# Cross attention for 16 batches: 718 keys in five tiles of 128 rows and one of 78, with the last tile's three products stacked into two

## The reference

```
query = hidden_states @ Wq                    # 100 x 640 per batch
keyt  = enc @ Wk                              # 718 x 640
valt  = enc @ Wv
scores = einsum('bhqd,bhkd->bhqk', qh, kh) * d ** -0.5
probs  = softmax(scores)
hs     = einsum('bhqk,bhkd->bhqd', probs, vh)
out    = (hs + ca_hs2) @ Wout + b_out + residual
```

## Time and profile before

| | |
|---|---|
| three runs | 1013.64 us median (1012.01 to 1024.04) |
| profiled execution | 1011.86 us, span 1010.1 us |
| TensorE (PE) busy | 988.2 us, 98% of the span |
| VectorE busy | 677.8 us, 67% |
| ScalarE busy | 489.2 us, 48% |
| GpSimd busy | 343.7 us, 34% |
| DMA | 190.12 MB, 188 GB/s on average |
| mean granted TensorE clock | 0.994 of full speed |

### The profile page before, as it was taken

The page is one execution under the profiler, slowest core; times in us unless marked ns, Lnnn a source line. Parts: engine busy times, 40 slices in busy tenths (PEclk is TensorE's granted clock), DMA queues, the critical chain, the costliest instruction groups (busy, mean ns, idle before and its releaser), DMA issues.

```text
span 1010.1 us, 20729 instructions
## 1 busy us (share of the span) xinstructions
PE 988.2 (98%) x6740; PEld 959.7 (95%) x6740; DVE 677.8 (67%) x1129; ACT 489.2 (48%) x895; POOL 343.7 (34%) x286
## 2 busy tenths in 40 slices
PE   9999899999999999999999999999999999999998
PEld 8998799999999999999999999999999999998997
DVE  6445586767776767676767776777767676766444
ACT  7434455454554545454636363645454545446110
POOL 5212253334242515161615243343333343406000
PEclk9999999999999999999999999999999999999999
DMA  7989967787879777879697878787787877795354
GB/s 264 255 298 272 250 154 198 157 201 168 189 167 195 169 191 171 183 176 186 169 186 184 187 176 190 178 184 187 166 201 162 199 169 190 156 219 160 98 177 148
DMA packets 154169, 190.12 MB, mean 188 GB/s; under 512 B 80928, under 2 KB 108192, under 8 KB 154144
## 3 DMA queue, kind: packets, MB, share of 16 engines
q1 hardware_dynamic: 147456, 177.44, 73.5%
q10 hardware_dynamic: 6688, 12.35, 3.7%
HBM read 81.56 MB, written 19.95 MB: 100 GB/s over the span
## 4 chain that ended last, share of the span: by engine, by line
PE 78%; DMA 7%; SPq 5%; DVE 4%; issue 2%; ACT 2%; POOL 1%; ACTq 0%; DVEq 0%; POOLq 0%
PE psS L750 20%; PE psB L785 19%; PE psB L790 9%; PE psS L725 7%; PE psT L766 6%; PE psS L894 6%; PE psT L812 4%; PE psT L818 2%; SPq L382 2%; DMA kstack<-kT 2%; DMA enc_raw<-in_encN_dram 1%; SPq L379 1%; PE psB L867 1%; PE psB L844 1%; PE psT L819 1%
## 5 line engine op out<-in xcount | busy, mean ns | idle before, releaser
L750 PE MATMUL psS<-encT_keep,Wk_keep 128*128 128x360 f32 x1440 | 253.8, 329 | 0.0
L750 PEld LDWEIGHTS psS<-encT_keep,Wk_keep 128*128 128x128 f32 x1440 | 237.4, 188 | 1.1 <-issue 0.4
L785 PE MATMUL psB<-PT_h,encN_h 120*128 120x400 f32 x576 | 202.3, 351 | 0.0
L785 PE MATMUL psB<-PT_l,encN_h 120*128 120x400 f32 x576 | 198.8, 345 | 0.0
L1133 ACT ACTIVATE probs<-psS,negmax 100x718 f32<-100x718 f32 x128 | 110.2, 861 | 133.5 <-DVE negmax L1524 133.4
L612 POOL TENSOR_TENSOR encT_keep<-encT_raw,encT_keep 128x718 fp32r<-128x718 f32 x45 | 79.7, 1772 | 199.6 <-ACT encT_keep L1162 197.3
L1548 DVE TENSOR_TENSOR kT<-psS,kT 128x718 fp32r<-128x718 f32 x80 | 72.4, 905 | 85.7 <-ACT kT L1157 85.6
L620 POOL TENSOR_TENSOR encN_l<-enc_raw,encN_h 120x768 fp32r<-120x768 f32 x48 | 93.1, 1940 | 90.9 <-ACT encN_h L1169 89.9
L790 PE MATMUL psB<-PT_h,encN_l 120*128 120x400 f32 x576 | 120.3, 344 | 0.8 <-POOL encN_l L620 0.8
L603 POOL TENSOR_TENSOR Mbd<-Mbd,fmask 128x320 fp32r<-128x320 f32 x48 | 46.7, 973 | 218.0 <-DMA Mbd<-m_split 215.4
L1157 ACT ACTIVATE kT<-psS 128x718 fp32r<-128x718 f32 x80 | 61.7, 771 | 115.7 <-PE psS L750 102.5
(11 more groups left out here) (245 smaller groups left out, 1642.2 us busy)
## 6 DMA issues: line engine op xcount, KB each, us to landing
kstack<-kT SPq DMA_DIRECT2D x64, 448.8 KB
kstack<-kT SPq DMA_DIRECT2D x192, 112.2 KB
enc_raw<-in_encN_dram SPq DMA_DIRECT2D x48, 360.0 KB, 5.5
encT_raw<-in_encT_dram SPq DMA_DIRECT2D x45, 359.0 KB, 4.4
kstack<-kT SPq DMA_DIRECT2D x32, 359.0 KB
kstack<-kT SPq DMA_DIRECT2D x32, 269.2 KB
kstack<-kT SPq DMA_DIRECT2D x32, 179.5 KB, 3.2
kstack<-kT SPq DMA_DIRECT2D x64, 89.8 KB, 3.5
```

The lines of the kernel that those rows point to most:

```text
L750: mm = pe.matmul(keys_in(f, first)[:, half, 0:HALF], w[:, c, f * 128:(f + 1) * 128], e[:, c, k0:k0 + HALF], start=(j == 0), stop=(j == 3 * ...
L785: pe.matmul(psB[:, 1, 0:RH], eN[0][:, k, cc], PT[p][:, k, rows], start=(k == 0 and p == 0), stop=False)
```

## The change

KP, the rows of a key tile, becomes 128 (KPAD 768), and the last tile holds 78 keys (TAIL). HALF, the width of a score half, stays 360. In a unit of `context` the first five tiles keep their 15 products. The three products of the last tile become two of 117 rows: the first takes high `encN` by high `PT` in rows 0 to 77 and, in rows 78 to 116, the first 39 rows of low `encN` by the first 39 of high `PT`; the second takes high `encN` by low `PT` and, in rows 78 to 116, the other 39 rows of low by high.

The rows 78 to 116 are filled by DMA, issued by SyncE in its order: `tail_pt` twice a batch (two DMAs of 39 rows x 400 columns each) and `tail_enc` once (two DMAs of 39 rows x 384 and one of 78 rows x 384). GpSimd makes the low part of the last tile first, in place in `enc_raw`, then of tile 4, then of tiles 0 and 1, 2 and 3. TensorE waits for `entail` and `pttail` ahead of the sixteenth matmul of a unit. At the end, GpSimd splits two parts of Wout instead of three ahead of the last `enc_low`, and `tail_pt(B - 1, 1)` stands ahead of the last stores and loads.

```
-KP = (KEYS + KT - 1) // KT
+KP = 128
 KPAD = KT * KP
-HALF = KPAD // 2
+HALF = 360
+FULLK = KEYS // KP
+TAIL = KEYS - FULLK * KP
+TH = TAIL // 2
+TSTK = TAIL + TH
...
+        tail_low = enc_raw[0:KP, FULLK * C:KT * C].bitcast(F32R)
...
+        def third(c):
+            return slice(4, 6) if c == 0 else slice(2 * (c - 1), 2 * c)
...  load_enc
-                    free("encN", PARTS * (b - 1) + c + 1, first)
-                    ks = slice(c * KQ, (c + 1) * KQ)
+                    free("encN", LOWS * (b - 1) + c + 2, first)
+                    if c == 0:
+                        free("entail", 48 * b, first)
+                    ks = third(c)
...
+                def tail_pt(b, half):
+                    wait_apart(sp, s["ptlo"], HEADS * b + 4 * half + 4, s["passed_sp"])
+                    rows = slice(half * RH, (half + 1) * RH)
+                    for p in range(2):
+                        sp.dma_start(raw(PT[p][TAIL:TSTK, FULLK, rows]),
+                                     raw(PT[0][p * TH:(p + 1) * TH, FULLK, rows])).then_inc(s["pttail"], 16)
+                def tail_enc(b):
+                    wait_apart(sp, s["encN"], LOWS * b + 1, s["passed_sp"])
+                    for p in range(2):
+                        sp.dma_start(raw(eN[p][TAIL:TSTK, FULLK, :]), raw(tail_low[p * TH:(p + 1) * TH, :]))\
+                          .then_inc(s["entail"], 16)
+                    sp.dma_start(raw(eN[1][0:TAIL, FULLK, :]), raw(eN[0][0:TAIL, FULLK, :])).then_inc(s["entail"], 16)
...  batch of SyncE, behind load_encT(i + 1, 1)
                     if not first:
+                        tail_pt(i - 1, 1)
                         store_hs(i - 1, 0)
...  batch of SyncE, behind load_x(i + 1)
                     if first:
                         sp.wait_ge(s["encT"], PARTS)
                         sp.dma_start(wv_raw, tiled(Wv)).then_inc(s["wvin"], 16)
                         load_q(i + 1)
-                    else:
+                    tail_pt(i, 0)
+                    tail_enc(i)
+                    if not first:
                         wait_apart(sp, s["hsp"], 2 * i, s["passed_sp"])
                         load_v2(i)
...  SyncE, the end
                 for t in range(2):
                     load_tile(0, t)
+                tail_pt(B - 1, 1)
                 store_hs(B - 2, 1)
...  enc_low of GpSimd
+                    pool.wait_ge(s["encNhi"], PARTS * b + 1)
+                    nc.gpsimd.tensor_tensor(tail_low, rawN[:, FULLK, :], eN[0][:, FULLK, :],
+                                            ALU.subtract).then_inc(s["encN"], 1)
+                    nc.gpsimd.tensor_tensor(eN[1][:, FULLK - 1, :], rawN[:, FULLK - 1, :], eN[0][:, FULLK - 1, :],
+                                            ALU.subtract).then_inc(s["encN"], 1)
...  context of TensorE
-                    for k in range(KT):
+                    for k in range(FULLK):
                         for p in range(2):
                             pe.matmul(psB[:, 1, 0:RH], eN[0][:, k, cc], PT[p][:, k, rows],
                                       start=(k == 0 and p == 0), stop=False)
-                    for k in range(KT):
-                        if u == 0 and k % KQ == 0:
-                            pe.wait_ge(s["encN"], PARTS * i + k // KQ + 1)
-                        mm = pe.matmul(psB[:, 1, 0:RH], eN[1][:, k, cc], PT[0][:, k, rows],
-                                       start=False, stop=(k == KT - 1))
-                    mm.then_inc(s["u"], 1)
+                    for n, k in enumerate((4, 0, 1, 2, 3)):
+                        if u == 0 and n in (0, 1, 3):
+                            pe.wait_ge(s["encN"], LOWS * i + (n + 1) // 2 + 2)
+                        pe.matmul(psB[:, 1, 0:RH], eN[1][:, k, cc], PT[0][:, k, rows], start=False, stop=False)
+                    if u == 0:
+                        pe.wait_ge(s["entail"], 48 * i + 48)
+                    if c == 0:
+                        pe.wait_ge(s["pttail"], 64 * i + 32 * half + 32)
+                    pe.matmul(psB[:, 1, 0:RH], eN[0][0:TSTK, FULLK, cc], PT[0][0:TSTK, FULLK, rows],
+                              start=False, stop=False)
+                    pe.matmul(psB[:, 1, 0:RH], eN[1][0:TSTK, FULLK, cc], PT[1][0:TSTK, FULLK, rows],
+                              start=False, stop=True).then_inc(s["u"], 1)
```

More of the change, by code:

```diff
@@ L109, in program @@
         NP = FT + 1
+        LOWS = PARTS + 1
         HALFCOLS = slice(GT, 2 * GT)
@@ L249, in program @@
         splits = "encT encN gbd ahi a xhi xlo v2bd mbd wolo passed_sp passed_pool"
+        tails = "pttail entail"
         stage1_loads = "xT0 xT1 xT2 xT3 xT4 wqin0 wqin1 wqin2 wqin3 wqin4 wgin cain wkcain wvcain wkin encin wvin hin"
@@ L256, in program @@
         stage1_stores = "qst0 qst1 qst2 qst3a qst3b v2st mst0 mst1 mst2"
-        names = " ".join((loads, products_done, exps_and_highs, steps_and_lows, splits, stage1_loads, stage1,
+        names = " ".join((loads, products_done, exps_and_highs, steps_and_lows, splits, tails, stage1_loads, stage1,
                           stage1_stores)).split()
@@ L547, in _ @@
                 batch(B - 1, last=True)
-                sp.wait_ge(s["encN"], PARTS * B)
+                sp.wait_ge(s["encN"], LOWS * B)
                 for t in range(2):
                     load_tile(0, t)
+                tail_pt(B - 1, 1)
                 store_hs(B - 2, 1)
@@ L616, in enc_low @@
                 def enc_low(b):
-                    for c in range(PARTS):
-                        ks = slice(c * KQ, (c + 1) * KQ)
+                    pool.wait_ge(s["encNhi"], PARTS * b + 1)
+                    nc.gpsimd.tensor_tensor(tail_low, rawN[:, FULLK, :], eN[0][:, FULLK, :],
+                                            ALU.subtract).then_inc(s["encN"], 1)
+                    pool.wait_ge(s["encN"], LOWS * b + 1)
+                    nc.gpsimd.tensor_tensor(eN[1][:, FULLK - 1, :], rawN[:, FULLK - 1, :], eN[0][:, FULLK - 1, :],
+                                            ALU.subtract).then_inc(s["encN"], 1)
+                    pool.wait_ge(s["encN"], LOWS * b + 2)
+                    for c in range(1, PARTS):
+                        ks = third(c)
                         pool.wait_ge(s["encNhi"], PARTS * b + c + 1)
@@ L621, in enc_low @@
                                                 ALU.subtract).then_inc(s["encN"], 1)
-                        pool.wait_ge(s["encN"], PARTS * b + c + 1)
+                        pool.wait_ge(s["encN"], LOWS * b + c + 2)
                 def spread_v2(b):
@@ L698, in wo_low @@
                     pool.wait_ge(s["wolo"], c + 1)
-                for c in range(3):
+                for c in range(2):
                     wo_low(c)
                 enc_low(B - 1)
-                for c in range(3, FT):
+                for c in range(2, FT):
                     wo_low(c)
```

## The result

| | before | after |
|---|---|---|
| median | 1014.28 us (1012.01 to 1024.04, 4 runs) | 1067.43 us (1064.1 to 1071.72, 4 runs) |
| ratio | | 1.0528, interval 1.0483 to 1.0573 |
| profiled execution | 1011.86 us, span 1010.1 | 1064.1 us, span 1062.4 |
| mean granted TensorE clock | 0.994 | 0.976 |

The change makes the kernel 5.3% slower: 47 us above the forecast of 1020 and above the upper end of its range, 1038. It is also above the slower rival's 1053.

What follows compares the result with a forecast made beforehand. TensorE's program order was taken to bound the kernel. 1011.9 - 17.6 + 13.1 + 6.5 + 5.4 + 0.3 = 1019.6, say 1020 us; the range leaving out 2 in 10 was 1003 to 1038.

Steps and rivals of the forecast that it cites:

- slower rival: Wait at context(i-1,3) becomes general and long enough to lower TensorE's clock: 1053 us; chance of over 1034, 0.15.
- Removed, -17.6: TensorE's context: 96 matmuls of 400 columns taken out at 0.183 us each, all on the path, 17.6 us.
- Shape, 0: Tiles of 128 rows instead of 120: matmuls cost nothing more, transposes 0 to 1 us, taken as 0.
- tail_enc and tail_pt(i, 0) in a middle batch. Cost 0: Five SyncE issues behind load_x land before context(i,0)'s sixteenth matmul; lift(i+1,0) is not delayed: 0 us.
- tail_pt(i-1, 1), +13.1: Second-half tail lands behind load_encT(i+1,1), so context(i-1,3)'s sixteenth matmul waits, mostly in 7 of 15 batches: +13.1 us.
- the bound of 30: Upper bound for waits at context(i-1,3): tail takes 2 us under load instead of 0.7 and every batch waits.
- Batch 0, +6.5: Five tail DMAs behind load_q(1) make context(0,0) wait 4.9 us, plus 1.6 of lower clock: +6.5, bounds 3 and 9.
- The end, +5.4: Near the kernel's end tile 2 lands later: 3.8 us of waiting plus 1.6 of lower clock, +5.4, bounds 1 and 9.
- The last enc_low, +0.3: TensorE starts 0.3 earlier and asks for low tiles 2 and 3 three matmuls earlier: +0.3 us.
- The gain beside the matmuls: GpSimd's shorter first instruction frees VectorE earlier in mid-batch, cutting TensorE waits: up to 5 us, 1015; no separate chance.

Runs made afterwards that it cites:

- no_tails: Changed kernel without the seven tail DMAs a batch and TensorE's waits for them: 995.34 us, ratio 0.9833 to the kernel before.
- only_middle: Changed kernel without the two DMAs for the second half of the heads and their wait, keeping the five in mid-batch: 1043.14 us, ratio 1.0306.
- experiments 5 and 6: Changed kernel with only the second-half tail DMAs, issued at the batch's head: 1021.95 us; complete changed kernel with those two issued by ScalarE: 1041.96 us.
- experiment 7: Complete changed kernel with load_v2's three DMAs issued by GpSimd instead of SyncE in batches 1 to 15: 1042.21 us, ratio 1.0265.
- the second half alone: Changed kernel with only the two tail DMAs for the second half of the heads and their wait: 1037.15 us, ratio 1.0269.

## Why the prediction was wrong

- **Removed, -17.6:** right. no_tails has 18.0 less than before (1013.36 - 995.34).
- **Shape, 0:** right, in both the context's distances and the transposes. Six transposes take 0.52 us at 120 and at 128 columns.
- **"tail_enc and tail_pt(i, 0) in a middle batch. Cost 0": this step failed.** It followed the five DMAs to TensorE's need for them, and there it was right: in only_middle the one wait for them among the larger entries is batch 0's. It then followed the queue behind them only as far as lift(i+1,0), called that not delayed, and ended. Two errors lie in it. The issues take 0.75 to 0.83 us, not 0.6 to 0.7, and with their gaps fill 4.2 us instead of 3.2. The prediction held to L382's shortest, 0.58, though the median in the same row is 0.785. There was no room for that: with the five ending at 549.5, load_v2 and store_hs, 3.2 us together, would have ended at 552.7, just ahead of the lift's 552.89, and 1 us more makes the lift late. It went out 1.4 us later behind load_x in the mean, and 2.4 late against TensorE in batch 8. And load_q stands behind lift(i+1,0), with 7.6 us from issue to need before, and a landing of 7.1 in the changed kernel: little slack, and the step never looked at it. Its price in the changed kernel is 25.9 us of waiting and some 13 of lost clock, where the sum had 0.
- **tail_pt(i-1, 1), +13.1:** the place and the mechanism were right: the tail lands 0.6 us behind the load, and an earlier issue cures the wait (experiments 5 and 6). In the changed kernel it waits 9.4 us in 9 places of up to 2.6, close to the forecast, but by luck: without the waits for q it is 23.5 (experiment 7). Alone it waits 23.3 us at 15 places instead of 13.1, nearly all of it in 7; that is inside the bound of 30 in waiting, but with the clock and the end it makes 42. The landings were read batch by batch from the one kernel in which they were short.
- **Batch 0, +6.5:** 5.7 us of wait against 4.9 forecast, but TensorE then stays at 0.50 until 144. (The 3.3 us of half speed don't follow from the earlier trace rows, whose 0.76 over 4 us is 1.9 us; but the next 4 us of that trace stood at 0.81, 1.5 more, which gives 3.4.)

```profile
136.00:138.00 2.00, 1.72 (x8) 1.61 (x8) 0.11 (x1) 0.51 (x1) 0.00 (x0) 0.50 0.91 228
...
142.00:144.00 2.00, 2.00 (x9) 2.00 (x8) 0.17 (x1) 0.00 (x0) 0.00 (x0) 0.52 0.00 0
144.00:146.00 2.00, 2.00 (x17) 1.98 (x17) 0.86 (x1) 1.67 (x3) 0.12 (x1) 1.00 0.00 0
```

That is 7.7 us of work at half speed, 3.9 lost instead of 1.6: together 9.6.

- **The end, +5.4:** the wait for tile 2 is 6.2 us instead of 3.8, and the clock is low again for some 3.4 us behind it (matmuls of 320 columns at 0.27 us instead of 0.15). Together about 8. The tile's load is issued 3.7 us behind the first tail's issue, where 3.4 were forecast; from its issue to VectorE's split go 7.5 us (985.30 to 992.83), where 5.2 were forecast. The landing under load was too short again.
- **The last enc_low, +0.3:** 1.3 us of wait against 0.8 before, +0.5.
- **The rivals:** the slower one had the right sign and, for the second half alone, the right mechanism, but no rival held a wait for a DMA that the change merely pushes back. Its open question, what a wait between 1.37 and 2.97 us does to the clock, has no single answer here: of the fourteen q waits, 0.93 to 2.70 us long, seven go with a low clock, the shortest of them 1.56 us, and a wait of 1.99 does not. The gain beside the matmuls did not show: norm's neighbours are no entry of the changed kernel's waits.

The chance of 0.15 for slower was too low for another reason as well: in the sum, the clock was charged to batch 0 and the end alone. Behind the q wait of 2.6 us in batch 8, the worst case, the clock loss was 3.1, more than the wait itself; over the kernel the busy time grew by half of what the idle time did (23.5 to 46.4).

The Trainium skill, "DMA: Bandwidth & Descriptors", section "Issuing engines are not separate DMA queues", says that spreading DMAs over engines saves only the sequencer's time to initiate them, which it calls usually small relative to the DMA. The first half agrees with the runs here. The second doesn't hold for this kernel: 0.75 to 0.83 us of issue against landings of 2.4 to 3.0, seven times a batch, and moving three issues of another load off SyncE is worth 25 us (1067 to 1042).

## What to carry to other kernels

Where one queue issues nearly all DMAs in program order, an added issue delays all that stand behind it up to the next point where the queue waits anyway: walk the queue on to that point, with the measured issue time of the same kind of DMA, and compare for each load the time from issue to need with its landing under load. Issues at a busy place go to another engine's queue, at a point where that engine is idle, or ahead of the large loads. And landings read in the old kernel need not hold in the new one: here their mean went from 4.8 us to between 6.3 and 8.2 with every edit. Take the long ones.

## What was not expected of the hardware

- An SBUF to SBUF issue of 39 rows holds SyncE for 0.74 to 0.84 us whether it moves 56, 384 or 400 columns. 78 rows of 384 columns take 0.77. The time of the issue doesn't go with the bytes. On GpSimd the three v2 issues took 1.83 us together, on SyncE 2.5.

```profile
L404 SPq DMA_DIRECT2D PT_h<-PT_h x32: 801/829/835, 130.5 to 981.6; - x32
L404 SPq DMA_DIRECT2D PT_l<-PT_h x32: 748/758/787, 131.3 to 982.4; - x32
...
L413 SPq DMA_DIRECT2D encN_l<-encN_h x16: 770/771/771, 133.8 to 963.2; - x16
```

- How long TensorE stays at 1.2 GHz behind a wait varies: 7.7 us of work behind 5.75 in batch 0, 6.3 behind 2.59 in batch 8, 3.4 behind 6.2 at the end. None follows behind seven q waits of 0.93 to 1.99 us. What decides it wasn't tried.
